# Expert lists built per pair of batches inside the attention, expert tiles started before the attention ends, and results added straight into the output

## The chip, the cores and the metric

The kernel runs on one core of a Trainium2 chip. The metric is device time in microseconds (us) for one execution, the median over several. The core's engines each run their own instruction stream and meet through semaphores: TensorE (PE), VectorE (DVE), ScalarE (ACT), GpSimd (POOL) and SyncE (SP). SP issues most DMAs; the indirect ones (rows gathered or scattered by an index) are issued by POOL.

## The reference

A gated cross-attention layer and then a gated mixture-of-experts layer, on x of 16 batches x 256 tokens x 256 features (4096 tokens).

```python
x = x + tanh(g_xattn[0]) * xattn(layernorm(x), ctx, ctx, Wq, bq, Wk, bk, Wv, bv, Wo, bo)   # 16 heads of 16
x = x + tanh(g_ffn[0])   * moe(layernorm(x), Wr, br, W1, b1, W2, b2)

def moe(xt, ...):                       # E = 8 experts, H = 1024, TOP_K = 2
    logits = xt @ Wr + br
    top_vals, top_idx = top_k(logits, 2)
    gate = softmax over the two chosen logits, 0 elsewhere
    h = relu(einsum('td,edh->teh', xt, W1) + b1)
    y = einsum('teh,ehd->ted', h, W2) + b2
    return einsum('ted,te->td', y, gate)
```

## The kernel before

**Attention** runs as a software pipeline over the 16 batches. A body m holds the row maxima of batch m (`scores_max`, `reduce`), the softmax and its product with the values of batch m-1 (`scores`, `exp`, `attend`), and the closing steps of batch m-2: `turn_out`, `attended_T`, `output`, `residual`, `norm2`, `norm2_T`. The router of batch m-3 stands there too; it writes eight logits per token into `logits`. Each body has eight steps (u on PE, v on ACT, w on DVE), and every engine's order is written out by hand. Bodies 4 to 13 are a hardware loop, the others are unrolled, up to body 17 (`NB + 1`), which only closes batch 15. The weights of six experts are cut into a high and a low fp16 part during the bodies; those of the last two (`LATE`, eight halves) follow in bodies 16 and 17 and after them, through `late_load` on SP, `late_high` on ACT and `late_low` on DVE. The residual rows go to `x1_d`, the normalized rows to `xn2_d`, both in DRAM.

**Routing** follows when all 4096 tokens have logits. DVE takes both maxima and one-hot masks over 256 columns (32 token groups x 8 experts). PE forms ranks with a triangular matmul (`tri`, `ones`). Then 64 rounds of `hot_row` and `hot_col` on DVE with a matmul each on PE invert the permutation: `slot_token` says which token stands in which slot, `slot_dest` to which row its result goes, `tile_expert` which expert owns which tile of 256 slots. There are 39 tiles, since each expert's last one may be partly empty.

**Expert tiles.** `tiles` runs step j as a pipeline: POOL gathers the rows of tile j+2, PE turns them (`gathered_T`), ACT and DVE cut them (`high_x`, `low_x`), PE does `first(j+1)`, ACT `relu`, DVE `cut_hidden`, PE `second(j-1)`, DVE `result(j-1)`, and POOL scatters the two halves (s = 0, 1) of a tile to `y_d`, where each (token, choice) has a row of its own. `first` and `second` are interleaved on PE chunk by chunk. No scatter waits for another.

**Combination.** When every scatter has landed (`y_sent`), SP loads `y_d` back in 16 pieces, DVE forms x1 + gate1 y1 + gate2 y2, and ACT's queue stores the output.

The waits are semaphores. `hold` is a wait on SP or POOL, and in a loop it is followed by an increment of `passed`. `link` on DVE waits for the instruction just issued.

## Time and profile before

| what | value |
|---|---|
| median of 3 runs | 956.3 us (951.59 to 957.45) |
| profiled execution, its own time | 956.5 us |
| its span, first to last instruction | 954.5 us |
| mean granted TensorE clock | 0.921 of full |
| busy share | PE 85%, DVE 61%, ACT 44%, POOL 39% |

The profiled execution is 2.0 us longer than its span and 0.2 us above the median, so sums over the span can be carried to the median by adding 2 us. Times in the trace count from the start of the span. Between two stretches the share of busy time differs so much that the page's totals say little: the stretches have to be read one by one.

### The profile page before, as it was taken

To read this page: it belongs to the slowest core of one execution; us is meant where nothing else is said; L and a number is where in the kernel's file an instruction comes from. 1 tells how busy PE (TensorE), PEld (TensorE's weight loads), DVE (VectorE), ACT (ScalarE), POOL (GpSimd) and SP (SyncE) were. 2 spreads that over 40 slices of the span, in tenths; PEclk is the share of its full clock that TensorE was granted. 3 is DMA by queue.
4 is the path that set the end of the run, shared out by engine and by line. 5 is a ranking of instruction groups with operands and counts; after the bars stand their busy time and mean duration, and the time that the engine had idled before them with its cause. 6 is when DMAs were issued, how large, how long until landed. Compare 5 with 4: busy or idle time off the path is not lost.

```text
span 954.5 us, 21547 instructions
## 1 busy us (share of the span) xinstructions
PE 809.2 (85%) x6484; PEld 554.4 (58%) x6485; DVE 586.1 (61%) x1015; ACT 416.5 (44%) x777; POOL 375.8 (39%) x399
## 2 busy tenths in 40 slices
PE   4589999999999998751579999999999999999920
PEld 3345655555555554330257777777777777777610
DVE  3466777777777777237945555555555555555547
ACT  2066677777776776421033333333333333333200
POOL 4113334343444423220033555555555555555210
PEclk9599999999999999755579999999999999999965
DMA  3335556556555552238011111111111111112069
GB/s 114 111 105 158 173 156 189 182 172 184 173 165 165 172 155 78 89 111 275 0 45 45 46 46 48 55 45 48 44 49 53 46 49 44 49 49 55 24 222 327
DMA packets 93936, 103.07 MB, mean 108 GB/s; under 512 B 9478, under 2 KB 80588, under 8 KB 93772
## 3 DMA queue, kind: packets, MB, share of 16 engines
q1 hardware_dynamic: 81900, 77.95, 26.4%
q0 software_dynamic: 7488, 20.46, 7.0%
q10 hardware_dynamic: 4512, 4.20, 1.3%
q8 instruction: 21, 0.34, 0.2%
q14 instruction: 15, 0.12, 0.0%
HBM read 67.03 MB, written 35.39 MB: 107 GB/s over the span
## 4 chain that ended last, share of the span: by engine, by line
PE 77%; DVE 6%; ACT 5%; issue 4%; DMA 3%; SPq 3%; POOL 1%; DVEq 0%; ACTq 0%; POOLq 0%
PE banks L1411 20%; PE banks L1258 8%; PE banks L1397 7%; PE banks L1398 7%; PE banks L1399 7%; PE banks L1184 7%; PE banks L1246 4%; PE banks L1213 3%; PE banks L1281 3%; PE banks L1225 2%; ACT probs L733 2%; PE banks L1165 2%; PE banks L1269 2%; PE banks L1384 2%; DVE hot_col L1061 1%
## 5 line engine op out<-in xcount | busy, mean ns | idle before, releaser
L1411 PE MATMUL banks<-wall,hh 128*128 x624 | 222.7, 379 | 0.5 <-DVE yb L1113 0.5
L808 ACT ACTIVATE hid<-banks,b_col 128x256 f32<-128x256 f32 x312 | 130.8, 470 | 209.2 <-PE banks L1399 113.7
L907 DVE TENSOR_REDUCE negmax<-banks 128x4 f32<-128x1024 f32 x128 | 155.8, 1217 | 54.0 <-PE banks L1225 52.8
L1397 PE MATMUL banks<-xh,wall 128*128 128x256 f16 x624 | 171.0, 274 | 0.0
L1398 PE MATMUL banks<-xl,wall 128*128 128x256 f16 x624 | 170.9, 274 | 0.0
L1399 PE MATMUL banks<-xh,wall 128*128 128x256 f16 x624 | 170.8, 274 | 0.0
L619 POOL DMA_INDIRECT y_rows<-yb,dest_idx x78 | 106.7, 1368 | 162.2 <-DVE yb L1113 124.5
L1411 PE MATMUL banks<-wall,hl 128*128 x624 | 157.4, 273 | 0.0
L733 ACT ACTIVATE probs<-banks 128x1024 f32<-128x1024 f32 x128 | 131.1, 1025 | 58.8 <-PE banks L1246 57.7
L1111 DVE SCALAR_TENSOR_TENSOR yb<-banks,b_b 128x256 f32<-128x256 f32 x78 | 33.1, 424 | 133.2 <-PE banks L1411 133.2
L1258 PE MATMUL banks<-probs,vaug 128*32 128x256 f32 x1024 | 84.0, 400 | 25.0 <-ACT probs L733 16.6
L1105 DVE TENSOR_TENSOR hl<-hid,hh 128x1024 f16<-128x1024 f32 x78 | 95.5, 1225 | 2.7
L609 POOL DMA_INDIRECT xg<-xn_rows,gather_idx x78 | 77.1, 989 | 48.2 <-issue 29.4
L570 POOL TENSOR_TENSOR xres<-xres,out_bias 128x512 f32<-128x512 f32 x16 | 20.3, 1270 | 168.3 <-DMA xres<-in_x 168.3
L1398 PEld LDWEIGHTS banks<-xl,wall 128*128 x624 | 61.3, 98 | 34.2
L1411 PEld LDWEIGHTS banks<-wall,hh 128*128 128x128 f16 x624 | 61.0, 98 | 34.7 <-issue 0.9
L1411 PEld LDWEIGHTS banks<-wall,hl 128*128 128x128 f16 x624 | 61.1, 98 | 15.5
L1397 PEld LDWEIGHTS banks<-xh,wall 128*128 x624 | 61.3, 98 | 8.0 <-issue 0.4
L1399 PEld LDWEIGHTS banks<-xh,wall 128*128 x624 | 61.4, 98 | 7.4
L798 ACT ACTIVATE xh<-banks 128x512 f16<-128x512 f32 x39 | 23.3, 597 | 93.5 <-PE banks L1384 93.5
L1225 PE MATMUL banks<-ks,qs 48*128 48x256 f16 x512 | 50.6, 276 | 13.2 <-DMA qs<-q_parts 7.1
L1094 DVE SCALAR_TENSOR_TENSOR xl<-banks,xh 128x512 f16<-128x512 f32 x39 | 27.0, 691 | 53.6 <-ACT xh L798 53.6
(160 smaller groups left out, 1193.5 us busy)
## 6 DMA issues: line engine op xcount, KB each, us to landing
wst<-in_L_ffn_W SPq DMA_DIRECT2D x32, 512.0 KB, 3.9
k_parts<-kparts SPq DMA_DIRECT2D x48, 128.0 KB, 2.4
ks<-k_parts SPq DMA_DIRECT2D x64, 96.0 KB, 2.4
q_parts<-qparts SPq DMA_DIRECT2D x48, 128.0 KB, 2.0
qs<-q_parts SPq DMA_DIRECT2D x64, 96.0 KB, 2.2
xin<-in_x SPq DMA_DIRECT2D x16, 256.0 KB, 4.7
cin<-in_ctx SPq DMA_DIRECT2D x16, 256.0 KB, 5.2
xres<-in_x SPq DMA_DIRECT2D x16, 256.0 KB, 3.0
```

Source lines behind the costliest of these rows:

```text
L609: nc.gpsimd.indirect_dma_start(xg[par][:, s, :], None, xn2_d, bass.IndirectOffsetOnAxis(gather_idx[par][:, s:s + 1], 0)).then_inc(xg_full[ ...
L619: nc.gpsimd.indirect_dma_start(y_d, bass.IndirectOffsetOnAxis(dest_idx[par][:, s:s + 1], 0), yb[par][:, s, :], None).then_inc(y_sent[par], 16)
L733: nc.scalar.activation(probs[v % 2][:].rearrange("p h t -> p (h t)"), banks[:, 2:4, :].rearrange("p b t -> p (b t)"), ACT.Exp, scale=float ...
L808: ins = nc.scalar.activation(hid[half][:, c % (HC // 2), :], banks[:, b, c % 2 * TS:(c % 2 + 1) * TS], ACT.Relu, bias=b1_col[:, ds(e * HC ...
L907: nc.vector.tensor_reduce(negmax[:, c, 8 * (g // 2):8 * (g // 2) + 8].rearrange("p (m g p2) -> p m g p2", m=2, g=2)[:, :, g % 2, :], banks ...
L1105: nc.vector.tensor_tensor(hl[par][:, cs, :], hid[half][:], hh[par][:, cs, :], ALU.subtract).then_inc(hl_ready, 1)
L1225: ins = nc.tensor.matmul(banks[:, j // 2, (j % 2) * L:(j % 2 + 1) * L], qs[par][r:r + KR, i, c * P:(c + 1) * P], ks[par][r:r + KR, i, :], ...
L1258: ins = nc.tensor.matmul(banks[32 * j:32 * j + 32, 7, 0:L], vaug[par][:, c, 8 * (j // 2) + 2 * g + j % 2, :], probs[v_ % 2][:, j, :], star ...
L1397: nc.tensor.matmul(dst, hi, xh[par][:, m, :], start=(m == 0), stop=False)
L1398: nc.tensor.matmul(dst, hi, xl[par][:, m, :], start=False, stop=False)
L1399: ins = nc.tensor.matmul(dst, lo, xh[par][:, m, :], start=False, stop=(m == M - 1))
L1411: ins = nc.tensor.matmul(dst, h_[:, c, s * P:(s + 1) * P], w_, start=(c == 0 and k == 0), stop=(c == HC - 1 and k == 1))
```

## The change

Three things are altered, with the arithmetic of a tile as it was.

1. **Lists.** The eight-expert table over all tokens is replaced by small steps on a pair of batches (4 token groups x 8 experts = 32 columns). They stand inside the bodies: in even bodies from 4 on (`listing`) DVE finds the two experts of each token, and PE forms ranks (`ranks`) from that pair plus a running `carry`; in odd bodies from 5 on (`gating`) DVE forms the places and gates, and POOL scatters (token, gate) pairs of 8 bytes into `list_d`, where each expert has a region of T rows (`enlist`, 8 indirect DMAs per pair).
2. **Early tiles.** After five pairs (10 of 16 batches) at least 13 full tiles exist whatever the routing. `early_table`, in body 15, lays out those 13, and body 16 already gathers tiles 0 and 1. Body 17 is gone from `bodies`; what it did for batch 15 is spread between the matmuls of the first two tiles. The lists of the last two pairs, the table of the other 26 tiles (`later_table`) and the search for a harmless row for empty slots (`fillers`) are placed in tile steps 0 to 5. SP loads each tile's slots from `list_d` (`slot_load`). The late weights are loaded from body 14 on and cut in bodies 15 and 16; the buffers of the tiles lie over attention buffers that are free by then.
3. **Results.** The attention's residual rows are stored to the output itself. A tile's result is multiplied by its gate on DVE (a third operation in `result`) and added to the output's rows by an accumulating indirect DMA. Since two tiles may hold the same token, each of the 78 scatters waits for the landing of the one before it. `y_d`, `x1_d`, the load back and the combination are gone.

The pieces of the diff are, in this order, of all engines, of POOL (the scatter, the start of the tiles, the lists), of DVE (the step of a tile) and of PE (behind the bodies).

```diff
-            for m in range(NB - 2, NB + 2):
+            for m in range(NB - 2, NB + 1):
                 body(m // 2, m % 2)
...
-            def scatter(j, par, s):
+            def scatter(j, par, s, lap):
                 hold(pool, y_ready, SUB * j + s + 1)
-                nc.gpsimd.indirect_dma_start(y_d, bass.IndirectOffsetOnAxis(dest_idx[par][:, s:s + 1], 0),
-                                             yb[par][:, s, :], None).then_inc(y_sent[par], 16)
+                if s == 0:
+                    hold(pool, dest_ready, j + 1)
+                    if isinstance(j, int) and j == 0:
+                        hold(pool, x1_stored, 16 * NB)
+                    wait(pool, y_sent[1 - par], 16 * SUB * (lap + par))
+                else:
+                    hold(pool, y_sent[par], 16 * (SUB * lap + 1))
+                nc.gpsimd.indirect_dma_start(out_rows, bass.IndirectOffsetOnAxis(dest_idx[par][:, s:s + 1], 0),
+                                             yb[par][:, s, :], None, compute_op=ALU.add).then_inc(y_sent[par], 16)
...
+            hold(pool, av_mm, 8 * (NB - 1))
+            hold(pool, xn2_stored, 16 * EARLY_PAIRS * 2)
             gather(0, 0, 0)
             gather(1, 0, 1)
-            hold(pool, lists_ready, 3)
+            residual(NB - 1)
+            tokens(NB // 2 - 2)
+            gather(2, 1, 0)
+            norm2(NB - 1)
+            gather(3, 1, 1)
+            enlist(NB // 2 - 2, 0)
+            enlist(NB // 2 - 2, 1)
...
+            def enlist(q, kk):
...
+                for i in range(PAIR):
+                    nc.gpsimd.indirect_dma_start(list_d, bass.IndirectOffsetOnAxis(place_i[:, kk, i:i + 1], 0),
+                                                 entry[:, kk, i, :], None).then_inc(list_sent, 16)
...
+                if fixed and j == 3:
+                    later_table()
                 if there(j, 1):
                     for half in range(2):
                         cut_hidden(j + 1, 1 - i, half)
+                if fixed and j == 0:
+                    router(NB - 1, 1, 7)
+                    listed_top(q)
+                elif fixed and j == TILE_LEAD - 1:
+                    fillers()
...
-            router(NB - 1)
+            n = NB - 1
+            router(n - 1, NB // 2 - 2)
+            pe.wait_ge(table_ready, 2)
             pe.wait_ge(late_lo, len(LATE))
             e = pe.value_load(tile_expert[0:1, 0:1], min_val=0, max_val=E - 1)
-            for c in range(HC):
+            first(0, 0, e, 0)
+            first(0, 0, e, 1)
+            turn_out(n, 0)
+            turn_out(n, 1)
+            for c in range(2, 6):
                 first(0, 0, e, c)
+            attended_T(n)
+            first(0, 0, e, 6)
+            first(0, 0, e, 7)
+            output(n, 0)
+            output(n, 1)
+            gathered_T(1, 0, 1)
```

The order on DVE in a looped body that lists, from its step 2 to its step 4. In rows of the order, `ISA` and `REGISTER_ALU` only prepare addresses and semaphore values. Before:

```order
L907 TENSOR_REDUCE negmax<-banks 128x2x2
L863 SCALAR_TENSOR_TENSOR qparts<-banks,qk_col,qparts 128x256 x2
L935 ISA
L936 ISA
L936 REGISTER_ALU
L936 SCALAR_TENSOR_TENSOR wall<-wst_113,wall 128x1024
L904 REGISTER_ALU
L907 TENSOR_REDUCE negmax<-banks 128x2x2
```

And now (`onehot`, `masked` and `best` are of the choice of experts):

```order
L1078 TENSOR_TENSOR onehot<-iota_e,index 128x32
L1009 REGISTER_ALU
L1012 TENSOR_REDUCE negmax<-banks 128x2x2
L947 REGISTER_ALU
L1082 SCALAR_TENSOR_TENSOR masked<-onehot,logits 128x32
L968 SCALAR_TENSOR_TENSOR qparts<-banks,qk_col,qparts 128x256 x2
L1040 ISA
L1041 ISA
L1041 REGISTER_ALU
L1041 SCALAR_TENSOR_TENSOR wall<-wst_157,wall 128x1024
L947 REGISTER_ALU
L1062 TENSOR_REDUCE best_70<-masked 128x4
```

Small operations stand between the reductions `negmax`, which PE waits for; the next `negmax` row follows directly behind these. A body that lists gains 14 of them and a body that gates 9.

The order on PE from the last step of the last full body to the first expert matmul. Before (`xg` are the gathered rows, `hot_col` and `hot_row` the inversion of the permutation):

```order
L1258 MATMUL banks<-probs_100,vaug_98 32x256 x4
L1165 MATMUL banks<-ident,xn2b 128x128 x4
L1296 MATMUL banks<-wr,x2T 128x8 x4
L1269 MATMUL banks<-ident,oT 128x2x64 x8
L1165 MATMUL banks<-ident,cn 128x128 x4
L1281 MATMUL banks<-wo,cT 128x256 x4
L1165 MATMUL banks<-ident,xn2b 128x128 x4
L1296 MATMUL banks<-wr,x2T 128x8 x4
L1369 MATMUL banks<-picked,tri 128x256
L1370 MATMUL banks<-picked,ones 128x256
L1374 MATMUL banks<-hot_col,hot_row 128x78 x64
L1384 MATMUL banks<-ident,xg_156 128x128 x4
```

And now:

```order
L1490 MATMUL banks<-probs_143,vaug_142 32x256 x4
L1557 MATMUL banks<-ident,xg_163 128x128 x4
L1478 MATMUL banks<-qs_140,ks_141 128x256 x4
L1490 MATMUL banks<-probs_144,vaug_142 32x256 x4
L1397 MATMUL banks<-ident,xn2b 128x128 x4
L1538 MATMUL banks<-picked,tri 128x32
L1540 MATMUL banks<-picked,ones 128x24
L1540 MATMUL banks<-picked,ones 128x16
L1540 MATMUL banks<-picked,ones 128x8
L1542 MATMUL banks<-carry,ones 128x32
L1530 MATMUL banks<-wr,x2T 128x8 x4
L1665 TENSOR_LOAD tile_expert
```

The gathered rows of tile 0 are turned inside the last body, ahead of that body's last scores, and the first expert matmul follows directly behind the router.

## Rows read from the trace of the kernel before

**Rows 1.** Busy time by stretch: start:end, length, engines (instructions), clock, DMA share, GB/s

```profile
209.00:231.50 22.50, 21.26 (x197) 13.11 (x196) 17.38 (x29) 16.09 (x27) 9.24 (x9) 1.00 0.56 172
386.00:408.00 22.00, 16.66 (x128) 7.79 (x126) 4.52 (x12) 12.17 (x17) 5.49 (x5) 0.73 0.16 55
431.00:486.00 55.00, 18.04 (x81) 9.54 (x82) 43.32 (x132) 3.33 (x6) 7.74 (x15) 0.50 0.37 124
486.00:912.00 426.00, 425.23 (x3268) 322.69 (x3266) 234.34 (x349) 153.34 (x350) 218.24 (x225) 1.00 0.15 46
912.00:955.00 43.00, 0.00 (x0) 0.00 (x0) 27.09 (x66) 0.00 (x0) 0.97 (x1) 0.55 0.88 299
```

**Rows 2.** Timeline of SP behind the last scatter: start, duration, operation

```profile
915.35 0.37 SPq L518 DMA_DIRECT2D y1b<-y_rows  x1
```

**Rows 3.** Timeline of PE: end of the bodies to the first expert matmul

```profile
404.58 1.08 PE L1258 MATMUL banks<-probs,vaug 128*32 128x256 f32 x8 [1.49 <-ACT oT L742]
...
410.13 1.87 PE L1296 MATMUL banks<-wr,x2T 128*128 128x8 f32 x8 [0.69 <-ACT x2T L702]
...
485.83 0.39 PE L1397 MATMUL banks<-xh,wall 128*128 128x256 f16 x1
```

**Rows 4.** Timeline of POOL: the norm at the end of body 16

```profile
403.76 2.43 POOL L552 TENSOR_SCALAR xn2b<-x1b,mean_var,rstd 128x256 f32<-128x256 f32 x2 [0.20 <-POOL rstd L547]
```

**Rows 5.** The chain of waits: a gather, and a scatter, from issue to landing

```profile
479.27 2.63 DMA xg<-xn_rows,gather_idx
...
912.91 2.42 DMA y_rows<-yb,dest_idx
```

**Rows 6.** Timeline of DVE in one looped body, and small routing operations

```profile
210.88 0.17 DVE L899 TENSOR_TENSOR logits<-banks,br_b 128x16 f32 x1 [1.90 <-PE banks L1296]
...
218.54 0.88 DVE L863 SCALAR_TENSOR_TENSOR qparts<-banks,qk_col,qparts 128x256 f16<-128x256 f32 x2 [0.70 <-ACT qparts L672]
...
220.47 1.22 DVE L907 TENSOR_REDUCE negmax<-banks 128x4 f32<-128x1024 f32 x1
...
223.56 1.20 DVE L907 TENSOR_REDUCE negmax<-banks 128x4 f32<-128x1024 f32 x1
...
446.75 0.17 DVE L1032 TENSOR_SCALAR e_int<-e_cnt 128x8 int32<-128x8 f32 x1
446.95 0.17 DVE L1033 TENSOR_SCALAR e_int<-e_int 128x8 int32<-128x8 int32 x1
```

**Rows 7.** Timeline of PE: reductions' readers in that body, and a bf16 matmul

```profile
221.74 0.39 PE L1225 MATMUL banks<-ks,qs 48*128 48x256 f16 x4
...
224.82 0.39 PE L1225 MATMUL banks<-ks,qs 48*128 48x256 f16 x4
...
443.93 0.39 PE L1369 MATMUL banks<-picked,tri 128*128 128x256 bf16 x1 [11.65 <-DVE picked L1019]
```

**Rows 8.** Timeline of POOL, a looped body, then a tile

```profile
216.37 1.27 POOL L570 TENSOR_TENSOR xres<-xres,out_bias 128x512 f32<-128x512 f32 x1 [10.36 <-DMA xres<-in_x]
...
603.68 0.98 POOL L619 DMA_INDIRECT y_rows<-yb,dest_idx  x1 [2.50 <-DVE yb L1113]
...
607.11 0.97 POOL L609 DMA_INDIRECT xg<-xn_rows,gather_idx  x1 [0.30 <-issue]
609.13 1.91 POOL L619 DMA_INDIRECT y_rows<-yb,dest_idx  x1 [1.06 <-DVE yb L1113]
```

**Rows 9.** Timeline of DVE in that tile, behind the result and beside the second scatter

```profile
607.88 0.42 DVE L1113 SCALAR_TENSOR_TENSOR yb<-banks,yb 128x256 f32<-128x256 f32 x1
608.22 0.68 DVE L1103 CAST hh<-hid 128x1024 f16<-128x1024 f32 x1
...
610.08 0.69 DVE L1103 CAST hh<-hid 128x1024 f16<-128x1024 f32 x1
```

**Rows 10.** The chain of waits in two neighbouring tiles: start, length, step

```profile
603.03 0.44 PE banks L1384 x4
...
613.91 0.44 PE banks L1384 x4
```

925 lines of the change are left out of this document (576 added, 349 removed).

## The prediction

> **What bounds the kernel now.** I read the busy time by stretch first [rows 1]. Three of its rows show two regimes and two holes. In an attention body (209 to 231.5 us) PE is busy 21.3 of 22.5 us; in the expert tiles (486 to 912) 425.2 of 426.0 us. PE is the bound in both. From 431 to 486 PE has 18.0 of 55 us at half the granted clock while DVE is busy for 43.3: routing. From 912 to the end PE has nothing and the DMA share is 0.88: the combination. In body 16 (386 to 408) PE is already down to 16.7 of 22 us. Then I read each seam where the change acts: PE's timeline from the last body to the first expert matmul [rows 3], POOL's norm there [rows 4], the end [rows 2], one attention body on DVE and PE [rows 6, 7], and one tile on POOL [rows 8, 9]. The gain can only come from the two holes and the closing of batch 15. The loss comes from whatever the new steps add to the two full stretches.
>
> **The combination goes.** SP starts the load back at 915.35, when the last scatter has landed [rows 2, 5]. The span ends at 954.5, so 39.15 us are removed. The new end is longer than the old one by the last two scatters, which now follow one another. Each takes (2.42 + D) us to land, D being what accumulating adds (below). With D = 1, a third operation on DVE and a second wake of POOL, the last row lands some 3.5 us later than at 915.35. Net **-35.7**.
>
> **The routing hole goes.** Before, the first expert matmul starts at 485.83 [rows 3]. After, its earliest time on the same time scale follows from POOL. The norm of batch 14 ends at 403.76 + 2.43 = 406.2 [rows 4]. The gather of tile 0 stands behind it: an index copy, a wait and two issues, the second landing 2.63 us after its issue [rows 5], so with the way from one POOL issue's end to the second gather's start (603.68 + 0.98 to 607.11, 2.45 us, rows 8) 406.2 + 2.45 + 2.63 = 411.3. PE needs these rows at its step 6, just behind the `attend` at 404.58 [rows 3], and waits there for some 5.5 us. Then come the turn, the last scores, exp and `attend`, the turn of `xn2b`, the rank matmuls and the router, with DVE's `low_x` ahead of the ranks' evacuation. Before, the way from that `attend` to the end of the body's router was 410.13 + 1.87 - 404.58 = 7.4 us; with the second scores and the 0.6 us steps of ACT between them I make it 9.8 us behind the gather: first expert matmul at **421**. That is **-64.8**. All of batch 15's closing work is thereby later than the first tile.
>
> **That closing work comes back on PE.** Between first(0) and the step in which first(2) and second(0) run together, PE does eight turns of `oT`, four of `cn`, eight matmuls of `output`, four turns of `xn2b` and a router. At full clock this is 6 us, and it waits three times. The longest wait is for DVE: `low_x(1)` stands behind attended, the first half of `cut_hidden`, residual, the statistics, six small steps and the other half of `cut_hidden` (1.86 us each half, the distance of the casts at 608.22 and 610.08, rows 9). I get 438.5 for first(1) and 447.3 for first(2). The two blocks of `first`, a turn and nothing else would have taken 10.8 us. From 421 to 447.3 are 26.3, so **+15.5**. The clock was at half or between in this place before (0.73 in body 16, 0.50 behind it, rows 1), and I add **+3** for first(0) at 1.2 GHz.
>
> **Table, lists and fillers in tile steps 1 to 5.** PE gets a rank product and eight one-column matmuls, 1.5 us. DVE gets about 60 small steps. A linked small step costs 0.20 us, the distance from 446.75 to 446.95 [rows 6], so 12 us over six tiles. DVE is busy in 234.3 of 426 us there [rows 1], so 4.9 of each 10.88 us [rows 10] are free and most of this hides. One place has no cover: at the end of step 5 PE waits for `passed_ready`, which stands behind `cut_hidden(6)` on DVE, and that ends 3.5 us into the next step (the cast at 610.08 and what follows it, with the turns at 603.03 and 613.91 as marks, rows 9 and 10). With nine small steps behind it, PE waits about 5.5 us, once. Other small delays 1. Together **+8**.
>
> **Small steps in the attention bodies.** This is the largest cost. DVE has slack at the start of a body (1.90 us before the logits) and 0.70 us before `qparts`, and then none: reduction 4 runs 220.47 to 221.69, and the scores that wait for it start at 221.74; reduction 5 runs 223.56 to 224.76, its reader starts at 224.82 [rows 6, 7]. Everything put ahead of these two falls on PE. In a listing body six steps stand before `qparts`, the last of them `masked`, and `best` stands behind the cut of the weights: seven times 0.20 is 1.4, less 0.70, is 0.7 us at reduction 4. Behind it come six more, 1.1 us, at reduction 5: 1.7 or 1.8 us. In a gating body the same count gives 1.2 - 0.7 = 0.5 and 0.3. The rank product on PE is five bf16 matmuls; at 0.1 to 0.2 us each (0.39 for 256 columns, rows 7) 0.6 us. A pair of bodies thus pays 3.0 us, six pairs **+18**. If DVE hides all of it, only 0.6 x 6 = 4 is left; if a step costs 0.25, it is 24. Body 15 also gets `early_table` (17 steps, 3.5 us, against 1.3 us of slack) and the cuts of three halves: +4. Body 16 has four conversions on ACT before its end instead of two: +1.5. Waiting for the new constants at the start: +0.5. Sum **+24**.
>
> **The list scatters** are 64 more indirect DMAs on POOL, eight in a row behind norm2 of a gating body. Eight times (0.97 + 0.30) is 10.2 us, and POOL sits idle for 10.36 us ahead of its next `xres` [rows 8]. I cost them at nothing; the cover is that idle time, and if the 8-byte rows issue slowly (1.91 instead of 0.97), 7 us spill and norm1 comes late for PE: 6 x 4 = 24 us.
>
> **The chain of result scatters** is where the change can fail. A scatter lands 2.42 us after its issue [rows 5] and POOL takes 0.83 us from an event of DVE to the next issue (608.30 to 609.13, rows 8 and 9), so one link is 3.25 + D. The second of a tile took 1.91 instead of 0.98 us on POOL while DVE ran the cast of `hh` beside it [rows 8, 9]: +0.93. Two links are 7.43 + 2D, a tile is 10.88 [rows 10], so D is free up to **1.72**. The trace has no accumulating transfer. Below, D is 0: it writes the same rows. Above, it reads like the gather (2.63 less the issue's 0.97, 1.66 us) before it writes and issues twice the descriptors, 0.97 more: 2.63. I take 1, nearer the plain scatter, since of the read only the latency comes on top. Then the chain is 9.4 us and hides. The gathers go between two scatters and fill the first link.
>
> Two pages bear on D. In the Trainium skill, Collectives: The Full Stack, section "The bandwidth ceiling", an add in a DMA costs a second source read and no more. With the fixed cost and rate of DMA: Bandwidth & Descriptors, "Anatomy of one DMA" (about 2.0 us and 436 GB/s), an estimate for 128 KB is 2.3 us plain, which the measured 2.42 supports, and 2.6 with the second read. D would be 0.3, the chain 8.0 us and the end 1.4 us earlier than in my sum.
>
> The lock between DVE's fast modes and POOL speaks against the change. What rows show is the 0.93 us above. SBUF — State Buffer, "SBUF: two separate sides", in the Trainium skill says that POOL can't write descriptors while DVE runs such an operation, as fp32 SBUF to SBUF. The new gate multiplication is one, twice per tile; by that rule each could add its own length of about 0.25 us to a link, and D would be free only up to 1.5.
>
> **Sum.** -35.7 - 64.8 + 15.5 + 3 + 8 + 24 = -50.0. The span becomes 904.5, the time **906** with the 2 us around it, and the median of the runs is as near the profiled one as before.
>
> **The rivals.** First, the insertions cost little: DVE's slack moves along with PE's waits, and only 8 of the 24 us and 18 of the 26.5 us (15.5 + 3 + 8) come. For it: ACT makes PE wait 1.5 us at the last `attend` anyway [rows 3]. Against it: two reductions without slack. Time 906 - 16 - 8.5 = **881**. Second, the early start is worth less: the eight late halves and the slot lists must pass SP in bodies 15 and 16 ahead of the max rows, and tile 0 starts 20 us later than 421. Time **926**. Third, on the other side: D = 2.63. Two links are 12.7 us, and every tile from the first scatter on takes 1.8 us more, 38 x 1.8 = 69, plus 3 at the end. POOL's wait holds its gathers too, so PE starves. Time **978**. It decides from D = 2.4 on, where the 50 us are eaten. Fourth, D around 2.1: 38 x 0.75 = 29, time **936**. That the change doesn't do what it says would show as a first tile behind the last router; I see no wait in PE's order that asks for it.
>
> **How the numbers follow.** Forecast 906 as reckoned 0.45; 881 0.18; 926 0.12; 936 0.10; 978 and worse, list scatters among them, 0.12; near nothing gained 0.03. A measurement of this kernel can tell about 1% from no change, 9.6 us. Faster by over 1% than 956.3 (below 946.7): 0.84; within: 0.04; slower: 0.12. The low end is 881 less 2 us for D = 0, less 5.5 for a gather that PE needn't wait for, less the rest of what DVE could hide, 4: 870. The high end takes in the fourth rival and the lower part of the third: 964.
>
> **What would show it.** The distance of two bodies should be 24 us instead of 22.6 in the loop, with waits of PE on `negmax` in steps 5 and 6. The first expert matmul should stand near 445 (421 + 24), the turns of tiles 10.9 us apart, and behind PE's last matmul there should be less than 10 us. If the turns are over 11 apart and POOL waits for its own DMAs, the chain bounds and D is over 1.7. If bodies stay at 22.6, DVE had slack that I don't see.

## The result, and the profile after

The changed kernel takes **931.3 us** (median of 4 runs, 928.86 to 934.43) against 956.9 us for the kernel before beside it; the ratio is 0.974 (95% interval 0.967 to 0.980). The forecast was 906 us. The profiled execution has a span of 927.6 us in 929.3.

The same stretches as in [rows 1] and their neighbours, from the windows of the changed kernel (columns as there):

```profile
158.40:189.30 30.90, 23.81 (x199) 14.09 (x197) 20.33 (x44) 16.02 (x27) 15.92 (x17) 0.89 0.70 138
209.00:231.50 22.50, 20.04 (x179) 12.54 (x180) 17.78 (x37) 15.42 (x25) 12.14 (x14) 1.00 0.74 173
431.00:486.00 55.00, 38.88 (x268) 30.07 (x269) 19.18 (x53) 15.30 (x34) 27.84 (x36) 0.74 0.24 62
486.00:600.00 114.00, 100.13 (x742) 74.37 (x740) 71.44 (x155) 34.04 (x79) 56.97 (x50) 0.94 0.31 41
600.00:900.00 300.00, 296.34 (x2280) 224.24 (x2278) 195.69 (x351) 106.58 (x244) 162.36 (x133) 1.00 0.30 47
900.00:927.60 27.60, 11.61 (x72) 6.67 (x69) 10.31 (x23) 0.84 (x2) 8.70 (x6) 0.80 0.26 29
```

The routing hole is filled (38.9 us of PE work in 431 to 486, 18.0 before) and the combination is gone. In return the same 22.5 us of the attention hold 20.0 us of PE work where they held 21.3, one body lasts 30.9 us, the first tiles leave PE idle for 14 of 114 us, and 27.6 us at the end hold 11.6 us of PE work. The DMA engines' share rose from 0.56 to 0.74 in the body and from 0.15 to 0.30 in the tiles, at nearly the same GB/s. What PE waited for, over the whole run (view of waits: us in total, times, longest):

```profile
...
PE banks L1557 <- DMA xg<-xn_rows,gather_idx: 15.3, 9, 6.5
PE banks L1457 <- DMA qs<-q_parts: 12.7, 5, 6.9
PE banks L1457 <- DVE negmax L1012: 8.4, 8, 2.4
...
PE banks L1710 <- DVE passed_by L1181: 7.1, 1, 7.1
...
PE banks L1478 <- DMA qs<-negmax_row: 5.9, 2, 4.4
PE banks L1570 <- DVE xl L1283: 5.5, 1, 5.5
...
PE banks L1570 <- issue: 1.7, 1, 1.7
```

Split into three parts, by PE's first expert matmul and its last matmul:

| part of the span | before | forecast | changed kernel |
|---|---|---|---|
| start to first expert matmul | 485.8 | 445 | 445.3 |
| first expert matmul to PE's last | 425.9 | 452.4 | 468.0 |
| PE's last matmul to the end | 42.8 | 7.1 | 14.3 |

(Forecast: 421 + 24; 425.9 + 15.5 + 3 + 8; 915.35 + 3.5 - 911.7.) The missing 23 us are in the second part (15.6) and the third (7.2). The first part came out to 0.3 us, but the experiments show that it did so for a wrong reason.

**Bodies.** The distance of two bodies is 22.6 us up to body 4. Then a gating body takes 22.6 to 22.8 us and a listing body 23.5 (the first), 30.9, 24.8, 25.6 and 24.6. In the body of 30.9 us the timeline of PE has its longest gap ahead of the scores that wait for a max row's transfer:

```profile
174.18 0.64 PE L1490 MATMUL banks<-probs,vaug 128*32 128x256 f32 x8
179.26 0.61 PE L1478 MATMUL banks<-qs,ks 49*128 49x256 f16 x4 [4.45 <-DMA qs<-negmax_row]
```

The DMA view of 164 to 184 us (KB each, median us to landing), and four windows of it, show what it waited for:

```profile
k_parts<-kparts SPq DMA_DIRECT2D x3, 128.0 KB, 11.8
q_parts<-qparts SPq DMA_DIRECT2D x3, 128.0 KB, 3.6
```

```profile
168.00:170.00 2.00, 2.00 (x24) 1.16 (x23) 1.93 (x7) 1.83 (x3) 1.61 (x2) 1.00 0.95 81
170.00:172.00 2.00, 2.00 (x22) 1.27 (x22) 1.51 (x3) 1.43 (x3) 0.96 (x1) 1.00 1.10 66
...
176.00:178.00 2.00, 0.00 (x0) 0.00 (x0) 1.86 (x6) 0.00 (x0) 0.00 (x0) 1.00 1.21 147
...
180.00:182.00 2.00, 0.53 (x4) 0.14 (x4) 0.41 (x2) 1.21 (x2) 0.00 (x0) 0.50 0.90 181
```

POOL issues its eight list scatters from 161.0 to 171.2. While they land, the engines are busy for all of the time with 66 to 81 GB/s, and the three stores of `kparts`, which land in 2.4 us in the kernel before (median), take 10.6 to 13.9. PE then waits for the loads of `qs` and `ks` behind them, and its clock is 0.50 behind the idle time.

**First tiles.** Turns of `xg` on PE mark the tiles. From the ninth on they are 10.9 us apart, but for six distances of 11.4 to 12.4; steps 3 to 5 take 14.2, 14.6 and 23.0 us. The timeline of PE there, and two windows behind it:

```profile
517.16 0.69 PE L1557 MATMUL banks<-ident,xg 128*128 128x128 f32 x2 [3.16 <-DMA xg<-xn_rows,gather_idx]
...
531.78 0.66 PE L1557 MATMUL banks<-ident,xg 128*128 128x128 f32 x4 [1.92 <-DMA xg<-xn_rows,gather_idx]
...
543.45 0.35 PE L1710 MATMUL banks<-ones,passed_by 128*128 128x1 bf16 x8 [7.10 <-DVE passed_by L1181]
545.50 0.39 PE L1570 MATMUL banks<-xh,wall 128*128 128x256 f16 x1 [1.69 <-issue]
...
554.81 0.60 PE L1557 MATMUL banks<-ident,xg 128*128 128x128 f32 x4
```

```profile
545.00:549.00 4.00, 3.50 (x15) 2.21 (x16) 0.00 (x0) 0.00 (x0) 0.00 (x0) 0.50 0.14 6
549.00:554.00 5.00, 5.00 (x32) 3.35 (x31) 0.00 (x0) 1.68 (x4) 0.00 (x0) 0.78 0.10 1
```

The fillers cost 7.1 us of waiting and 1.7 more behind it. The 3.3 us that are left of 23.0 - 10.9 fall in the stretch at the lower clock.

**The end.** The timeline of POOL. The result scatters (before: 0.98 or 1.91 us on POOL and 2.42 to land [rows 5, 8]) take 1.55 us or, beside DVE's cast, 2.4, and each is issued 4.5 to 5.3 us behind the one before:

```profile
903.20 2.43 POOL L689 DMA_INDIRECT out_dram<-yb,dest_idx  x1 [3.10 <-DMA out_dram<-yb,dest_idx]
908.46 1.54 POOL L689 DMA_INDIRECT out_dram<-yb,dest_idx  x1 [2.83 <-DMA out_dram<-yb,dest_idx]
913.07 1.55 POOL L689 DMA_INDIRECT out_dram<-yb,dest_idx  x1 [3.07 <-DVE yb L1344]
917.69 1.54 POOL L689 DMA_INDIRECT out_dram<-yb,dest_idx  x1 [3.08 <-DMA out_dram<-yb,dest_idx]
922.23 1.55 POOL L689 DMA_INDIRECT out_dram<-yb,dest_idx  x1 [3.00 <-DMA out_dram<-yb,dest_idx]
```

DVE beside the first of them:

```profile
904.12 0.69 DVE L1292 CAST hh<-hid 128x1024 f16<-128x1024 f32 x1
```

A scatter that adds lands 3.8 us after its issue (median of 78, 3.7 to 4.5); D is 1.4. PE's last matmul ends at 913.3, and from then on the last three scatters alone set the end.

### The profile page after: what moved, and what is told of

It is laid out like the page before. It is cut to its first block, busy times and chain, and to the rows that moved or that the text cites. A ratio compares the mean times of both kernels' runs of the same rounds, so it can differ in the third digit from the quotient of the medians.

```text
span 927.6 us, 22335 instructions
## 1 busy us (share of the span) xinstructions
PE 812.4 (88%) x6472; PEld 554.4 (60%) x6473; DVE 600.6 (65%) x1209; ACT 416.2 (45%) x784; POOL 443.6 (48%) x453
## 3 DMA queue, kind: packets, MB, share of 16 engines
q0 software_dynamic: 17024, 20.53, 14.4%
## 4 chain that ended last, share of the span: by engine, by line
PE 48%; DMA 22%; issue 11%; DVE 8%; POOL 5%; ACT 3%; SPq 2%; POOLq 1%; DVEq 0%; ACTq 0%
DMA out_dram<-yb,dest_idx 14%; PE banks L1584 11%; PE banks L1416 5%; PE banks L1490 5%; DMA qs<-q_parts 4%; PE banks L1570 4%; PE banks L1571 4%; PE banks L1572 4%; PE banks L1478 3%; PE banks L1445 2%; PE banks L1457 2%; PE banks L1397 2%; DMA xg<-xn_rows,gather_idx 2%; PE banks L1513 2%; ACT probs L829 1%
## 5 line engine op out<-in xcount | busy, mean ns | idle before, releaser
L689 POOL DMA_INDIRECT out_dram<-yb,dest_idx x78 | 134.5, 1724 | 167.9 <-DMA out_dram<-yb,dest_idx 74.2
L1570 PE MATMUL banks<-xh,wall 128*128 128x256 f16 x624 | 173.1, 277 | 8.1 <-DVE xl L1283 5.5
L1571 PE MATMUL banks<-xl,wall 128*128 128x256 f16 x624 | 173.2, 278 | 0.0
L1572 PE MATMUL banks<-xh,wall 128*128 128x256 f16 x624 | 173.1, 277 | 0.0
L677 POOL DMA_INDIRECT xg<-xn_rows,gather_idx x78 | 89.5, 1147 | 45.8 <-issue 23.8
L1490 PE MATMUL banks<-probs,vaug 128*32 128x256 f32 x1024 | 86.9, 413 | 23.7 <-ACT probs L829 16.8
L648 POOL DMA_INDIRECT token_lists<-entry,place_i x64 | 66.3, 1036 | 18.7 <-issue 18.7
L1478 PE MATMUL banks<-qs,ks 49*128 49x256 f16 x512 | 52.4, 285 | 5.9 <-DMA qs<-negmax_row 5.9
```

The lines of the kernel that those rows point to most:

```text
L677: nc.gpsimd.indirect_dma_start(xg[par][:, s, :], None, rows, bass.IndirectOffsetOnAxis(gather_idx[par][:, s:s + 1], 0)).then_inc(xg_full[p ...
L689: nc.gpsimd.indirect_dma_start(out_rows, bass.IndirectOffsetOnAxis(dest_idx[par][:, s:s + 1], 0), yb[par][:, s, :], None, compute_op=ALU.a ...
L1478: ins = nc.tensor.matmul(banks[:, 2 + j // 2, (j % 2) * L:(j % 2 + 1) * L], ks[par][r:r + KR + 1, i, c * P:(c + 1) * P], qs[par][r:r + KR ...
L1490: ins = nc.tensor.matmul(banks[32 * j:32 * j + 32, 7, 0:L], vaug[par][:, c, 8 * (j // 2) + 2 * g + j % 2, :], probs[v_ % 2][:, j, :], star ...
L1570: nc.tensor.matmul(dst, hi, xh[par][:, m, :], start=(m == 0), stop=False)
L1571: nc.tensor.matmul(dst, hi, xl[par][:, m, :], start=False, stop=False)
```

## The experiments

In the tables below, "first" is the start of the first expert matmul in the profiled run, "tiles" the time from there to PE's last matmul, "end" what follows. Medians are of all runs of a kernel, the three parts of its profiled run alone, which can be off the median: by 7.2 us in e8 (918.5 against 911.3), 5.4 in e5, 5.0 in e13. A group of runs was measured on one occasion, with the kernel before beside it. e1, e2, e7 and e15 leave out work that the output needs and only serve to measure.

**The chain of result scatters, the halves of the lists, the fillers** (one occasion, before 957.1 us).

```diff
 # e1: the result scatter
-    yb[par][:, s, :], None, compute_op=ALU.add)
+    yb[par][:, s, :], None)
 # e2: e1, and a table for each buffer
-    wait(pool, y_sent[1 - par], ...)  /  hold(pool, y_sent[par], ...)
-    indirect_dma_start(out_rows, ...
+    indirect_dma_start(y_d[2 * par + s], ...
 # e3: POOL, gating body t, then the listing body behind it
     enlist(t - 2, 0)
-    enlist(t - 2, 1)
+elif lists_at(m, par, LEAD):
+    enlist(t - 3, 1)
 # e4: TILE_LEAD = 8; DVE up to passed_by at the end of step 5,
 #     PE's eight matmuls and DVE's rest at the end of step 6
```

> The changed kernel (931.3 us) with one word of the result scatter left out: it writes its rows without adding them, so the output holds only one contribution to each row. All its waits stay. Theory A, the add makes the chain as long as a tile: in the changed kernel a scatter lands 3.8 us after its issue and holds POOL for 1.6 us, against 2.42 and 0.97 in the kernel before, and two links with the gather between them are 10.9 us, so what POOL is behind after step 5 is never made up. Without the add the landing goes back to 2.4 us, the four scatters that end the program one after the other become two, and the 6 us that the tiles lose from the eleventh on come back: 931 - 6 - 5 = 920 us, 917 to 923. Theory B, the chain is a bystander and the time was lost in the bodies and at the fillers: only the last two links get shorter, by 3 us, 928 us.

> As the kernel with the plain scatter, and the chain is gone too: each of the four row buffers is scattered into a table of its own, and no scatter waits for the one before it. The output is not filled. Theory A, a plain link of 3.25 us has slack in a tile of 10.9: nothing changes in the tiles against the plain scatter, and the end is one link, 3 us, shorter: 917 us. Theory B, it is the wait itself on POOL, which holds the next gather back at the steps with list scatters (PE waits 3.2 and 1.9 us for its rows in steps 3 and 4), that costs: another 5 us less than that, 912 us.

> Only the place of list scatters in the attention is changed: the four of the first choice stay behind the second norm of the gating body, the four of the second choice go behind the second norm of the body after it. Theory A, the 8 scatters of 128 rows of 8 bytes fill the DMA engines (DMA share 1.09 to 1.15 of the engines behind them, 0.4 to 0.5 there in the kernel before), and the parts of the queries and keys land late: bodies of 30.9, 24.8, 25.6 and 24.6 us instead of 22.6. With four at a time the worst waits go: bodies of 23 to 24 us, the body of 30.9 above all, in total 6 to 10 us less, 921 to 925 us. Theory B, my prediction's: the small steps on DVE make these bodies long; they are all still there, so 931 us within 1.5, and the same four bodies stay long.

> The last part of the table, the fillers, is cut in two: DVE's part before PE stays at the end of step 5, PE's eight one-column matmuls go to the end of step 6 instead of step 5, DVE's rest behind them, and eight steps instead of six are written out ahead of the loop. Theory A, PE's wait of 7.1 us for the last comparison of DVE, the 1.7 us behind it and the lower granted clock that follows it (0.50 for 4 us) are all that makes that step 23.0 us instead of 10.9: they go, 12 us less, 919 us. Theory B, the chain of scatters stands behind it: POOL is behind after the list scatters in steps 3 and 4 and used PE's stall to catch up; then the time that PE no longer waits there comes back as waits for rows or for room in the following steps, and 5 us or less are gained, 926 us or more.

| kernel | median us | ratio to before | first | tiles | end |
|---|---|---|---|---|---|
| e1 plain scatter | 956.3 | 0.997 (0.994 to 1.001) | 476.5 | 471.5 | 7.9 |
| e2 no chain | 952.6 | 0.995 (0.992 to 0.998) | 473.0 | 472.2 | 5.3 |
| e3 lists halved | 941.1 | 0.984 (0.980 to 0.988) | 449.6 | 475.2 | 13.8 |
| e4 fillers later | 957.6 | 1.000 (0.997 to 1.003) | 473.9 | 469.8 | 14.4 |

No theory had room for this: three kernels that have the changed kernel's attention, instruction for instruction, came 28 to 31 us later to the first expert matmul than it had (473.0 to 476.5 against 445.3). Their listing bodies took 31 to 34 us each, all but the first, which no list scatter precedes. The absolute forecasts of e1, e2 and e4 therefore failed, and they can be read only against the changed kernel measured again.

**The changed kernel again, and what stands in its bodies** (one occasion, before 955.5 us).

```diff
 # c0: nothing
 # e5: in the bodies, eleven small steps of DVE written twice, as
     top_equal(q, 0)
+    top_equal(q, 0)
 # e6: fillers in steps 7 and 8, TILE_LEAD = 10, and in POOL's step
     scatter(j - 2, i, 1, t - 1)
+    if 3 <= j <= 6: enlist(7, (j - 3) // 2), two of its four scatters
     scatter(j - 1, 1 - i, 0, ...)
-    if j in (3, 4): enlist(7, j - 3)
 # e7: no list scatter in a body; result to a scratch table
-    enlist(t - 2, 0)
-    enlist(t - 2, 1)
```

> The changed kernel itself, with nothing altered, beside the others on their chip. Three kernels that differ from it in the tiles alone came out at 953 to 958 us, and their profiles differ from the changed kernel's first in the attention, where the code is the same: bodies of 31.4, 32.0 and 31.6 us in place of 24.8, 25.6 and 24.6. Theory A, how far the list scatters hold the other transfers up is not a property of the code but of where or when it runs: this run shows bodies of 31 us too and 955 us. Theory B, something in the altered kernels did it after all: 931 us and bodies of 25.

> The small steps of DVE in the attention bodies are written twice where that changes nothing: eight more in a listing body, three more in a gating one (11 per pair of bodies, against 24 such steps in the changed kernel), so 0.20 us x 11 = 2.2 us more of DVE per pair. Theory A, the prediction's: there is no slack ahead of reductions 4 and 5, each pair of bodies pays 2 us more, 12 us over six pairs, beside the unaltered changed kernel of the same chip. Theory B: DVE waits for PE, which waits for transfers, and the steps lie in that wait: within 3 us of the changed kernel, and gating bodies still 22.6 to 23.

> Two edits in the first tiles. The last pair's eight list scatters go two by two between the two result scatters of steps 3 to 6, instead of four by four behind them in steps 3 and 4; the fillers are made at the end of steps 7 and 8 instead of step 5, with ten steps written out. Theory A, the gathers of tiles 6 and 7 stood behind four list scatters each: the steps of 15 and 16 us become 11 to 12, the filler step 11 to 12.6 (it was 12.6 in the kernel with only the fillers moved): 8 us less than that kernel's place, some 15 to 18 us less than the changed kernel on the same chip, less what the chain of result scatters takes back. Theory B, the chain bounds: the sum of the steps from the first tile to the sixteenth stays within 4 us of that of the kernel with only the fillers moved.

> The list scatters of the first six pairs, all those in the attention bodies, are left out (the lists then hold filler numbers in their places, and the result goes to a scratch table, so the output lacks the experts' part); every small step of DVE, the rank products on PE, the token steps of POOL and their waits are kept. Only the attention is read from it. Theory A, the transfers: every body from the sixth on is 22.6 to 23.5 us, the first expert matmul stands 8 to 20 us earlier than with the lists, at 425 to 437 in its profile. Theory B, the small steps: bodies of 23.5 to 24.5 us in pairs of 2 to 3 us more than 45.2.

| kernel | median us | ratio to before | first | tiles | end |
|---|---|---|---|---|---|
| c0 changed, again | 964.8 | 1.011 (1.007 to 1.014) | 469.5 | 478.3 | 15.0 |
| e5 small steps doubled | 969.1 | 1.014 (1.010 to 1.018) | 480.4 | 478.9 | 13.5 |
| e6 last lists spread | 942.8 | 0.987 (0.984 to 0.991) | 468.0 | 457.5 | 13.5 |
| e7 no lists in bodies | 913.4 | 0.956 (0.951 to 0.960) | 425.5 | 473.9 | 13.5 |

c0 settles that the alterations didn't do it: the changed kernel itself now takes 964.8 us, 1.1% more than the kernel before, with listing bodies of 30 to 32 us. That is Theory A of c0, which had 955. A window of it, rows of waits (PE over 160 to 400 us) and one row of DVE, in a listing body of 30 us:

```profile
272.00:281.00 9.00, 3.59 (x33) 2.75 (x32) 1.54 (x5) 2.04 (x5) 5.02 (x6) 0.76 1.05 177
```

```profile
PE banks L1501 <- DVE logits L1004: 22.7, 4, 5.9
PE banks L1490 <- ACT probs L829: 10.7, 10, 2.6
```

```profile
280.08 0.17 DVE L1004 TENSOR_TENSOR logits<-banks,br_b 128x16 f32<-128x16 f32 x1 [7.42 <-remote]
```

POOL issues list scatters from 268.5 to 278.5, the DMA share over the window is 1.05, and PE, ACT and DVE do nearly nothing from 275 to 280. DVE's idle time has no releaser that the profile names. e7 shows whose work this is: with the list scatters left out, and every small step, rank product and wait kept, bodies are 23.2 and 22.6 us in turn. The turn of `cin` on PE in four bodies running:

```profile
159.21 0.66 PE L1400 MATMUL banks<-ident,cin 128*128 128x128 f32 x4
...
182.46 0.66 PE L1400 MATMUL banks<-ident,cin 128*128 128x128 f32 x4
...
205.04 0.66 PE L1400 MATMUL banks<-ident,cin 128*128 128x128 f32 x4
...
228.22 0.66 PE L1400 MATMUL banks<-ident,cin 128*128 128x128 f32 x4
```

Without the 48 list scatters of the bodies the first expert matmul is 44 us earlier here (469.5 - 425.5) and 20 earlier than in the first measurement (445.3 - 425.5); the small steps and rank products cost 0.6 us per pair of bodies, where I had 3.0. Theory A holds for e7. e5 isn't clean: its median is 4.3 us over c0, between its theories (12, or at most 3), its profiled run 10, and the difference lies in listing bodies that are long for the other reason. One body can be read: body 4, ahead of any list scatter, is 25.7 us instead of 23.5. (Of the eleven doubled steps nine stand in a listing body and two in a gating one, not eight and three.) Nine steps for 2.2 us there, so the first helping of small steps fits mostly into DVE's slack and the next does not. Theory A's cost per pair is supported by this one body and not shown further.

e6 has c0's level in the attention and 20.8 us less in the tiles; its steps 3 to 5, 14.6, 15.8 and 23.0 us in c0, are 10.9, 12.4 and 10.9. Theory A. The fillers alone (e4) are 8.5 of it (478.3 - 469.8), with their step at 12.6 us; that lies between e4's two theories (12 or at most 5). Against c0 the plain scatter of e1 has 6.8 us less in the tiles and 7.1 at the end, near Theory A's 6 and 5; without the chain (e2) the end is 2.6 shorter still and the tiles no shorter, again Theory A. e3's gain, 941 us, is to be read with care, since the level of the attention moves by itself: its listing bodies are 24 to 26 us, but its gating bodies are now 23.4 to 27.5, so part of the stalls has gone where the scatters went.

The two levels, the cheaper of 931.3 us and the costlier of 964.8, show in one more place, tile step 0, beside the seventh pair's list scatters. The distance of the turns of `xg` there is 14.1 us in the changed kernel's first measurement and 21.3 to 21.5 in c0, e5, e6 and in e1 to e4. In c0, a window and PE behind it:

```profile
497.00:502.00 5.00, 0.00 (x0) 0.00 (x0) 0.00 (x0) 0.85 (x4) 2.60 (x3) 0.65 0.02 1
```

```profile
503.00 1.88 PE L1530 MATMUL banks<-wr,x2T 128*128 128x8 f32 x8 [7.80 <-ACT x2T L784]
```

PE and DVE do nothing for 5 us while POOL issues list scatters, and the DMA share is 0.02. So full DMA engines, which go with the body of 30.9 us, don't explain this stall. By the same mark e3 ran at the costlier level. There e1, e2 and e4, of its occasion, have their first expert matmul 23 to 27 us later than e3's 449.6, so halving the lists may have given that much; it isn't shown.

**Where the lists go, and what they write** (one occasion, before 956.9 us).

```diff
 # e8
-list_d = dram("token_lists", (LISTED, 2), F32)
-entry = sb("entry", [P, 2, PAIR, 2], F32)
+list_d = dram("token_lists", (LISTED, 16), F32)
+entry = sb("entry", [P, 2, PAIR, 16], F32)
 # e11: POOL in a body; the second choice from a copy
     norm1(m + 2, par)
+    enlist(t - 3, 1) if listing else enlist(t - 3, 0)
     norm2(m - 2)
-    enlist(t - 2, 0)
-    enlist(t - 2, 1)
 # e12: e11 and e6.  c1: nothing
```

> The changed kernel with list rows that are 64 bytes apart and written whole: each list scatter writes 128 rows of 64 bytes instead of 8, to its own aligned place, and the first filling of the lists is 2.2 MB instead of 0.28. All places and orders stay. Theory A, it is the writes of 8 bytes, several of which share 64 bytes, that block a DMA engine for 2 to 3.7 us at a time (single packets of 1 and 2 KB took up to 3.7 us beside list scatters and under 1.1 us in the kernel without them): with whole rows the bodies of 31 us fall to 23 to 24, the first expert matmul stands before 440 instead of 469.5, and the time is 930 us or less. Theory B, it is the number of rows that GpSimd's queue writes: nothing changes but the start, 965 us within 4.

> The list scatters of a pair of batches go one pair of bodies later and, four at a time, between POOL's two norms, the first choice in the listing body, the second in the gating one (from copies, since the step before overwrites them); in the changed kernel's profile the DMA engines are idle there (share 0.32, 0.00, 0.00 from 255 to 261), whereas behind the second norm the loads of the next batch run (0.8 to 1.1). The first round writes filler rows. All 8 scatters of a pair are still issued. Theory A, what costs is that they meet the loads and stores of the body's start: bodies of 23.2 to 24.2 and 22.6 to 23.6 us, first expert matmul at 430 to 436, 925 to 932 us. Theory B, a list scatter blocks whatever comes next wherever it stands: as with the lists halved, bodies of 24 to 26, first expert matmul near 450, 941 us.

> Both remedies together: list scatters between the norms in the attention, the last pair's two by two between the result scatters of steps 3 to 6, fillers in steps 7 and 8. Theory A, the two costs are independent (965 to 943 us by the tile part, 965 to 930 by the attention part): 908 us, 903 to 913, below both kernels, and near my forecast of 906. Theory B, the chain of result scatters becomes the bound as soon as PE no longer waits elsewhere: 918 us or more, with turns of tiles over 11 us throughout.

> The changed kernel once more, unaltered, as the measure for the other three of this call: 931 us as in its first measurement or 965 us as in its second. Theory A, the difference is the chip's: the run stands near one of the two and not between, and all its executions agree within 0.5%. Theory B, the time drifts from run to run: something between, spread over more than 1%.

| kernel | median us | ratio to before | first | tiles | end |
|---|---|---|---|---|---|
| c1 changed, third | 932.0 | 0.974 (0.969 to 0.979) | 442.0 | 473.3 | 14.5 |
| e8 rows of 64 bytes | 911.3 | 0.950 (0.946 to 0.955) | 431.0 | 471.8 | 14.0 |
| e11 lists between norms | 965.2 | 1.007 (1.003 to 1.010) | 476.1 | 478.4 | 13.5 |
| e12 both | 939.6 | 0.983 (0.978 to 0.987) | 477.0 | 448.2 | 13.0 |

c1 is back at 932 us, its four runs within 0.5% of that, and it ran on the chip on which e1, e2 and e4 had shown bodies of 31 us. So the level is neither fixed to a chip nor to the code. Within one occasion the runs of a kernel agree (within 0.8% of their median); what differs from one occasion to the next wasn't found. Where the program's tensors come to lie in memory is one candidate, and no run tested it.

e8 is the answer to what costs: the same 64 list scatters in the same places, each now writing eight times as much, to rows of its own, and the looped bodies are as without any, 23.2 and 22.6 to 22.9 us. Theory A. The first expert matmul is 11 us earlier than c1's and the median 20.7 us lower. Its waits of PE over 160 to 400 us have no transfer left, and `q1`, the queue of the loads and stores (packets, MB, share of the engines' time, 150 to 400 us), took less time for more data than in the changed kernel:

```profile
PE banks L1494 <- ACT probs L833: 9.9, 11, 0.9
PE banks L1461 <- DVE negmax L1016: 2.8, 6, 0.5
```

```profile
q1 hardware_dynamic: 41652, 40.24, 51.8%
```

```profile
q1 hardware_dynamic: 40096, 39.03, 59.8%
```

(The first is e8's, the second the changed kernel's.) Single packets of 1 or 2 KB in that queue last up to 1.1 us in e8 and up to 3.6 in the changed kernel. All kernels with rows 64 bytes apart were measured on this occasion and the next; the changed kernel was at its cheaper level on this one and wasn't run on the next, so that such rows also hold at the costlier level isn't shown.

e11 failed through my own edit. Four scatters between the norms hold POOL for 5 us, and the second norm is what PE's turn waits for, in its row of waits over 160 to 400 us:

```profile
PE banks L1416 <- POOL xn2b L597: 23.7, 9, 3.4
```

I had read the gap between the norms from a DMA share of 0.00 and not from POOL, where it is 0.3 to 1.5 us in the changed kernel and 2.7 in e7. The bodies are 26.5 to 28.5 us with the scatters away from the loads, and whether place alone would have helped stays open. e12 carries that loss too, but its tiles are 30 us shorter than e11's and 10.9 us apart nearly throughout: neither of its theories, since A counted on the gain in the attention and B on turns over 11.

**What in a row, and the rest of the tiles** (one occasion, before 956.4 us).

```diff
 # e13: e8 and e6
 # e14: e8, rows 64 bytes apart, of which a scatter writes 8
-    entry[:, kk, i, :], None)
+    entry[:, kk, i, 0:2], None)
 # e15: e13 with e1's edit
 # e16: e13, and the gather's index copy moved
-    nc.gpsimd.tensor_copy(gather_idx[par], slots[...])   (POOL, gather(j))
+    nc.vector.tensor_copy(gather_idx[1 - i], slots[...]) (DVE, step j, tile j + 3)
```

> List rows of 64 bytes, and in the first tiles the last pair's list scatters two by two between the result scatters of steps 3 to 6, the fillers in steps 7 and 8. Theory A, the two costs add up: in the profile with 64-byte rows steps 5 to 7 of the tiles took 13.1, 15.8 and 23.0 us; with 10.9, 12.4 and 10.9 in their place (as with 8-byte rows and the same edit) 17 us go: 911 - 17 = 894 us. Theory B, the chain of result scatters takes them back: 900 us or more.

> The list rows stay 64 bytes apart, but a list scatter writes only the first 8 bytes of each. Theory A, what blocks is that rows written by different DMA engines share 64 bytes: no two rows share them here, so 911 us as with whole rows, and no packet beside a list scatter longer than 1.2 us. Theory B, what blocks is a write of less than 64 bytes: 932 us or more, bodies of 25 to 31 us, packets of over 3 us.

> The kernel with 64-byte rows and the spread first tiles, and the result scatters write without adding (the output keeps one contribution per row). Theory A, the add costs two things: the end, where the last scatters follow one another (14.3 us between PE's last matmul and the end of the span; the plain ones make it 9 or less), and the single tiles of 11.4 to 12.6 us from the twelfth on (together 8 us in the profile with 64-byte rows), which the plain chain does not have: 10 to 13 us less than the same kernel with the add, 882 us. Theory B, those longer tiles come from something else (the gathers or a loop's turn): only 4 to 5 us less, 889 us.

> The kernel with 64-byte rows and the spread first tiles, and the copy of the gather's row numbers to whole numbers goes from POOL (0.75 us, then a wait of 0.3 to 1.0 us, once per tile) to DVE, a step ahead. Theory A, POOL's round of two scatters, a copy and two gathers is 10.9 us with the add and has no slack, so that each delay stays: with 1.7 us less it catches up, and the end comes 3 to 5 us earlier than without this edit. Theory B, the two links of the chain alone (3.8 us landing and 0.75 to the next issue) set the round: no difference, within 1 us.

| kernel | median us | ratio to before | first | tiles | end |
|---|---|---|---|---|---|
| e13 rows of 64 and spread | 891.9 | 0.933 (0.930 to 0.936) | 430.2 | 451.0 | 14.0 |
| e14 64 apart, 8 written | 914.7 | 0.954 (0.951 to 0.958) | 430.2 | 471.0 | 14.5 |
| e15 e13, plain scatter | 887.1 | 0.927 (0.925 to 0.929) | 429.0 | 449.4 | 9.7 |
| e16 e13, index on DVE | 885.3 | 0.925 (0.923 to 0.928) | 428.8 | 444.5 | 13.2 |

e14: Theory A. Its bodies are 23.2 to 23.6 and 22.6 to 22.8 us and its longest packet of 1 or 2 KB takes 1.2 us, so writing 8 bytes is no trouble when rows are 64 bytes apart; no distance between 8 and 64 was run. e13: Theory A, the two costs add up (911.3 - 891.9 = 19.4). e15: 4.9 us less, of which 4.3 at the end, is Theory B's number. Its reason doesn't hold: the single longer tiles inside the loop (11.7 and 12.0 us in e13) are gone, as Theory A had it, but the last two tiles that turn rows take 13.3 and 12.6 us (11.7 and 10.9 in e13), and what holds POOL's gather back there I did not trace. The end of e15 on POOL shows the plain link, 3.2 us, under the adding one's 4.6:

```profile
878.20 0.96 POOL L695 DMA_INDIRECT out_dram<-yb,dest_idx  x1 [4.22 <-DVE yb L1353]
881.40 0.96 POOL L695 DMA_INDIRECT out_dram<-yb,dest_idx  x1 [2.24 <-DMA out_dram<-yb,dest_idx]
884.56 0.96 POOL L695 DMA_INDIRECT out_dram<-yb,dest_idx  x1 [2.20 <-DMA out_dram<-yb,dest_idx]
```

e16: Theory A, and more than I gave it, 6.6 us. POOL's round with an adding scatter is two scatters (1.6 us each), a copy with its wait (1.8), two gathers (2.9) and a wait for the landing (3.5) against 10.9 us of tile; in the changed kernel one scatter starts 5.2 us behind the last, and the copy and the gathers stretch the other link to 5.7, which is the whole tile. With the copy on DVE the tiles are 10.9 us apart from the twelfth to the last, and 885.3 us is the fastest of all: 7.5% under the kernel before.

## Why the prediction was wrong

Two kinds of error have to be kept apart. The mechanism that failed is in the attention, where two wrong terms nearly cancelled. The 23 us by which the sum missed are in the first tiles and at the end.

**The list scatters** are the step that failed: "I cost them at nothing; the cover is that idle time". The cover on POOL was there, 10.4 us for 10.2, and it held. It was the wrong resource: the issues were free, the transfers of the other queues beside them were not. The scatters cost 14 to 20 us in the first measurement (445.3 against 431.0 with whole rows and 425.5 with none), 38 to 44 in the second, 11 to 16 in c1. Whole rows aren't free to the last us either: e13's last looped body is 1.2 us earlier than e7's, its first expert matmul 4.7 later (430.2). Half of that arises in body 15, at a lower clock for the same 174 matmuls (windows, e7's first):

```profile
365.20:385.50 20.30, 17.10 (x174) 9.49 (x174) 17.17 (x33) 13.03 (x21) 6.64 (x9) 1.00 0.53 177
```

```profile
364.00:387.40 23.40, 21.07 (x174) 12.10 (x174) 17.36 (x33) 13.09 (x21) 6.07 (x9) 0.78 0.46 154
```

Whether the scatters have a share in that clock isn't shown.

The rival in which they cost 24 us named late issue on POOL, which did not happen. Two signs were within reach before: the stretch of the body has a DMA share of 0.56 [rows 1], so the engines were half full, and the 8-byte row had no transfer in the trace from which to cost it. Like D it wanted a bound, and it got none.

**Small steps in the attention bodies** (+18 for six pairs): 0.6 us per pair, the rank product's size, so about 4. DVE's steps fitted into slack that I had not seen in the two reductions without idle time ahead of them; where exactly it lies I did not trace. (The working's 1.7, 0.8 and 0.6 us per pair add up to 3.1 and not 3.0, under 1 us in all.) The first rival, "the insertions cost little", was right for this half. The two errors cancelled by luck, and the first expert matmul stood at 445.3 on a forecast of 445: a landmark that fits is no proof of the terms in it. For bodies 15 and 16 I had +5.5: the way from the last turn of `cin` to the end of the norm ahead of tile 0's gather (67.9 us before) is 1.1 us longer in e7, 7.1 in e13 and 8.7 in the changed kernel.

**The routing hole** (-64.8): right. With the shift of 4.3 us at the last body's turn of `cin` in e7, 421 becomes 425.3, and e7 has 425.5. The gather of tile 0 was the last wait, 6.5 us for the 5.5 that I reckoned.

**Closing work and clock** (+15.5, +3): first(1) starts at 461.4 for 462.5, behind DVE's `low_x` as described, and first(2) at 472.8 for 471.3, or 474.3 with the clock's 3. Right within 2 us.

**Table, lists and fillers** (+8): mis-sized. The one uncovered place is the one I named, and its wait was 8.8 us instead of 5.5; the 3.3 us at the lower clock behind it, and the two gathers that stood behind four list scatters each on POOL, 3.3 and 3.7 us, were not in the sum. These are 19 us beyond three plain tiles (14.2, 14.6 and 23.0 against 10.9 each), and e6 (against c0) and e13 (against e8) give 20.8 us back where I had 8. This is the largest part, 11 us, of the 23 that the sum missed.

**The chain of result scatters**: D = 1 was 1.4, and the point from which it decides, 1.72, was not reached. But the issue itself is 0.6 us longer as well, so a link is 4.6 and not 4.25, two are 9.2, and what lies between them on POOL, which I let hide in the first link, made the round 10.9 us: exactly a tile, with nothing to make up a delay. A scatter chain that fits isn't one that can catch up. That and its single longer tiles are 6.8 us (e1 against c0, whose step 0 is the same 21.3 us), and at the end it leaves three scatters in a row instead of two.

**The combination** (-35.7): the end is 14.3 us behind PE's last matmul and not 7.1; the 35.7 were 28.5. By the page Collectives: The Full Stack of the Trainium skill, section "The bandwidth ceiling", an add is a second source read only, which gave an estimate of 2.6 us to land; the measured 3.8 decides against it here. By the Trainium skill, SBUF — State Buffer, section "SBUF: two separate sides", POOL can't write a DMA's descriptors while DVE runs in a two-port mode, as in a copy of fp32 within SBUF; the trace agrees, with the scatter of 2.43 us on POOL beside DVE's cast and 1.54 without it.

In all: 0.3 up to the first expert matmul, 15.6 in the tiles and 7.2 at the end are 23.1 us, the distance of 904.5 to the span of 927.6. With whole list rows and the first tiles' lists and fillers spread (e13) the change gives 891.9 us: the change could do more than I forecast and did less.

## What to carry to other kernels

An issue that costs its engine nothing still writes somewhere: cost the destination too, and give each short row that a scatter writes 64 bytes of its own, the distance that helped here. A serial chain that just fits its period turns every delay ahead of it into lost time, so look for what can leave the chain's engine before counting it as hidden. Measure a kernel on more than one occasion, the unaltered one beside the experiments, before reading a difference of a few per cent.

## What was not expected of the hardware

- Beside indirect scatters of 128 rows of 8 bytes that lie 8 bytes apart, the transfers of other queues take far longer: 128 KB that land in 2.4 us took up to 13.9, and a listing body grew from 23.2 to between 23.9 and 34. With rows 64 bytes apart the looped bodies are as without list scatters, whether 64 bytes are written (e8) or 8 (e14).
- How much that costs fell into two groups. The first expert matmul is 16 to 20 us behind e7's in two profiles (442.0 and 445.3) and 42 to 51 in five (468.0 to 476.5): 931.3 and 932.0 against 964.8 us for one kernel, its runs each time within 0.5% of the median. In the costlier case DVE is idle for up to 8.4 us with no releaser in the profile, and PE and ACT wait with it, once with a DMA share of 0.02. Why is open.
- An accumulating scatter of 128 KB lands in 3.8 us and holds POOL for 1.55 (plain: 2.42 and 0.97).
- Behind 8.8 us in which PE had only eight short matmuls its granted clock was 0.50 for 4 us, so that the price of a stall is more than the stall.
